# Attention's loop: where the two halves of a score tile stand in TensorE's step

## The reference, cut to what matters

```python
h = _modulate(_layernorm(x), shift_msa, scale_msa)
qkv = h @ W_qkv + b_qkv
q, k, v = (qkv[:, :, 0], qkv[:, :, 1], qkv[:, :, 2])
scores = jnp.einsum('blhd,bmhd->bhlm', q * scale, k)
attn = jax.nn.softmax(scores, axis=-1)
o = jnp.einsum('bhlm,bmhd->blhd', attn, v).reshape(b, l, c)
```

## Time and profile before

| | us |
|---|---|
| time, median of 3 runs | 3148.11 (3144.75 to 3148.4) |
| profiled execution, its own time | 3139.54 |
| its span, first to last instruction | 3137.9 |
| attention's head loop, about | 675 to 1762 of the span |
| first matmul of "scores" to the last | 673.5 to 1755.8 |

### The profile page before, as it was taken

The page is one execution under the profiler, slowest core; times in us unless marked ns, Lnnn a source line. Parts: engine busy times, 40 slices in busy tenths (PEclk is TensorE's granted clock), DMA queues, the critical chain, the costliest instruction groups (busy, mean ns, idle before and its releaser), DMA issues. The chain is left out here.

```text
span 3137.9 us, 51594 instructions
## 1 busy us (share of the span) xinstructions
PE 2823.0 (90%) x16066; PEld 2289.3 (73%) x16066; DVE 1682.8 (54%) x3405; ACT 1450.7 (46%) x1863; POOL 1434.5 (46%) x1065
## 2 busy tenths in 40 slices
PE   7769999979999999999999678689999999999976
PEld 3258787846666666666666467579999999999965
DVE  4456766669998998999899355401111111111125
ACT  2122322249999999999999445511111111111112
POOL 1232323138888888888888544412222222222200
PEclk9779999979999999999999788789999999999988
DMA  6376666644334333343343357792112111111153
GB/s 202 131 262 212 234 217 218 221 116 92 85 87 94 79 92 90 84 92 86 86 93 80 127 171 219 216 320 72 37 37 72 37 37 55 54 37 38 50 163 134
DMA packets 340331, 378.73 MB, mean 121 GB/s; under 512 B 167008, under 2 KB 230120, under 8 KB 340188
## 3 DMA queue, kind: packets, MB, share of 16 engines
q1 hardware_dynamic: 330588, 357.71, 38.3%
q0 software_dynamic: 4224, 9.44, 1.7%
q10 hardware_dynamic: 5380, 9.66, 1.0%
HBM read 226.82 MB, written 158.93 MB: 123 GB/s over the span
## 5 line engine op out<-in xcount | busy, mean ns | idle before, releaser
L815 POOL TENSOR_TENSOR a_pl<-a_pf,a_ph 128x1024 fp32r<-128x1024 f32 x384 | 909.8, 2408 | 23.1 <-ACT a_pf L912 22.9
L843 DVE TENSOR_REDUCE a_mx<-a_psum_s 128x1 f32<-128x512 f32 x992 | 637.8, 684 | 92.4 <-PE a_psum_s L941 88.6
L910 ACT ACTIVATE a_ph<-a_psum_t 128x1024 fp32r<-128x1024 f32 x512 | 526.6, 1028 | 116.2 <-PE a_psum_t L958 108.9
L1562 PE MATMUL m_psum_h<-m_ht,m_w 128*128 128x256 f32 x4032 | 534.9, 284 | 30.3 <-DMA m_w<-w_s 21.0
L1514 POOL TENSOR_TENSOR m_al<-m_af,m_ah 128x256 fp32r<-128x256 f32 x288 | 212.9, 739 | 762.7 <-DVE m_ah L1523 762.7
L1523 DVE CAST m_ah<-m_af 128x256 fp32r<-128x256 f32 x288 | 84.6, 294 | 848.4 <-ACT m_af L1500 848.4
L1562 PEld LDWEIGHTS m_psum_h<-m_ht,m_w 128*128 128x128 f32 x4032 | 508.8, 189 | 34.0 <-issue 33.1
L1500 ACT ACTIVATE m_af<-m_psum_h,m_bias 128x256 f32<-128x256 f32 x288 | 137.3, 477 | 814.2 <-PE m_psum_h L1562 814.2
L1576 PE MATMUL m_psum_y<-m_w,m_ah 128*128 128x288 f32 x2304 | 504.2, 296 | 1.4 <-DVE m_y L1540 1.2
L977 PE MATMUL a_psum_o<-a_ph,a_vs 128*100 128x512 f32 x1024 | 420.0, 410 | 23.8 <-POOL a_pl L815 19.7
L978 PE MATMUL a_psum_o<-a_pl,a_vs 128*100 128x512 f32 x1024 | 404.3, 395 | 0.0
(11 more groups left out here) (225 smaller groups left out, 3106.0 us busy)
## 6 DMA issues: line engine op xcount, KB each, us to landing
a_qs<-q_s SPq DMA_DIRECT2D x192, 144.0 KB
a_ks<-k_s SPq DMA_DIRECT2D x192, 144.0 KB
w_s<-q_ws SPq DMA_DIRECT2D x64, 324.0 KB, 3.4
h_s<-p_ht SPq DMA_DIRECT2D x40, 512.0 KB, 5.1
m_ht<-h_s SPq DMA_DIRECT2D x16, 1280.0 KB, 7.8
v_s<-q_vo SPq DMA_DIRECT2D x64, 288.0 KB, 2.3
a_vs<-v_s SPq DMA_DIRECT2D x128, 144.0 KB, 4.5
q_s<-q_qko SPq DMA_DIRECT2D x32, 512.0 KB, 2.8
```

The source lines that it names most:

```text
L815: pool.tensor_tensor(pl[:, s % RING], pf[:, s % RING], raw(ph[:, s % RING]), ALU.subtract).then_inc(lo_pool, 1)
L843: dve.tensor_reduce(mx[:, u % 2, t, h:h + 1], p_s[:, h * 512:(h + 1) * 512], AX.X, ALU.max) \
L910: act.activation(ph[:, s % RING], p_t[:, s % 2], ACT.Exp, scale=SCALE)
L1562: m = pe.matmul(p_h[:, f % RING, 0:GM], w1[:, k, f * P:(f + 1) * P], ht[:, q, a], start=(i == 0), stop=(i == len(PASSES) - 1))
```

## The change

TensorE's step is written in another order. Before, both halves of score tile s followed the four value products. Now half h0 is the first product of the step, ahead of the scores, and half h1 stands between the value products of the step's first key tile and those of its second. Number, size and operands of the products are the same, and so are all waits; they stand at other places. No other engine's list is changed.

```diff
-                def score_tile(hd, u, i, t):
-                    if t == 0:
+                def score_half(hd, u, i, t, h):
+                    if t == 0 and h == 0:
                         pe.wait_ge(qk_in[u], 16 * QK_LOADS * (i + 1))
-                    for h in range(2):
-                        pe.wait_ge(half_free, 2 * (KT * (hd - 2) + t) + h + 1)
-                        pe.matmul(p_s[:, h * 512:(h + 1) * 512], qs[0:SROWS, u, t * P:(t + 1) * P],
+                    pe.wait_ge(half_free, 2 * (KT * (hd - 2) + t) + h + 1)
+                    pe.matmul(p_s[:, h * 512:(h + 1) * 512], qs[0:SROWS, u, t * P:(t + 1) * P],
...
-                def values(hd, u, i, s):
+                def values(hd, u, i, s, r):
...
+                        ahead = not (last and u >= SLOTS - 2)
+                        tile = (hd + 2, (u + 2) % SLOTS, i + (u + 2) // SLOTS, s)
+                        if ahead:
+                            score_half(*tile, 0)
                         if s + AHEAD < STEPS:
                             scores(hd, u, i, s + AHEAD)
                         elif not (last and u == SLOTS - 1):
                             scores(hd + 1, (u + 1) % SLOTS, i + (u == SLOTS - 1), s + AHEAD - STEPS)
-                        values(hd, u, i, s)
-                        if not (last and u >= SLOTS - 2):
-                            score_tile(hd + 2, (u + 2) % SLOTS, i + (u + 2) // SLOTS, s)
+                        values(hd, u, i, s, 0)
+                        if ahead:
+                            score_half(*tile, 1)
+                        values(hd, u, i, s, 1)
```

More of the change, by code:

```diff
@@ L933, in lead_tile @@
                     score_product(lead_slots[n % 3], u, t)
-                def score_tile(hd, u, i, t):
-                    if t == 0:
+                def score_half(hd, u, i, t, h):
+                    if t == 0 and h == 0:
                         pe.wait_ge(qk_in[u], 16 * QK_LOADS * (i + 1))
-                    for h in range(2):
-                        pe.wait_ge(half_free, 2 * (KT * (hd - 2) + t) + h + 1)
-                        pe.matmul(p_s[:, h * 512:(h + 1) * 512], qs[0:SROWS, u, t * P:(t + 1) * P],
-                                  ks[0:SROWS, u, h * 512:(h + 1) * 512], start=True, stop=True) \
-                          .then_inc(half_ready, 1)
+                    pe.wait_ge(half_free, 2 * (KT * (hd - 2) + t) + h + 1)
+                    pe.matmul(p_s[:, h * 512:(h + 1) * 512], qs[0:SROWS, u, t * P:(t + 1) * P],
+                              ks[0:SROWS, u, h * 512:(h + 1) * 512], start=True, stop=True) \
+                      .then_inc(half_ready, 1)
                 def scores(hd, u, i, s):
@@ L960, in scores @@
                     m.then_inc(t_ready, 1)
-                def values(hd, u, i, s):
+                def values(hd, u, i, s, r):
                     lh, j = divmod(s, PER_LH)
-                    if s == 0:
+                    if s == 0 and r == 0:
                         pe.wait_ge(v_in[u], 16 * V_LOADS * (i + 1))
-                    if j == 0:
+                    if j == 0 and r == 0:
                         pe.wait_ge(o_copied[lh], START + hd)
[L969 to L980, removed]
+                    if r == 0:
+                        n_pool, n_dve = lo_counts(hd, s)
+                        if s in DVE_LO:
+                            pe.wait_ge(lo_dve, n_dve)
+                        else:
+                            pe.wait_ge(lo_pool, n_pool)
+                    t = PAIR * j + r
+                    cols = slice(r * GT, (r + 1) * GT)
+                    pe.matmul(p_o[0:VW, lh], vs[:, u, t], ph[:, s % RING, cols], start=(t == 0), stop=False)
+                    m = pe.matmul(p_o[0:VW, lh], vs[:, u, t], pl[:, s % RING, cols], start=False,
+                                  stop=(t == KT - 1))
+                    if r == PAIR - 1:
+                        m.then_inc(p_free, 1)
                 for n in range(LEAD):
```

## The result

The changed kernel takes **3217.97 us** (median of 4 runs, 3215.41 to 3220.84) where the kernel before takes 3146.43 beside it: a ratio of **1.023**, 95% interval 1.0212 to 1.0247. The forecast was 3213, in a range of 3185 to 3232. All times and ratios here are of runs in the faster of two states; one execution among the experiments, of the kernel with h0 behind the scores in steps 0 and 4, took 10397 us and is left out of them.

The account below looks back on a forecast made before the run. No engine alone but a ring of dependences was taken to set the pace; 47 heads at +0.90 and 14 boundary heads at +1.58 us gave 64.4, which from the median 3148.1 made 3213, range 3185 to 3232.

Parts of the forecast that it names:

- The ring before: Dependences from POOL's split through its low parts, TensorE and DVE back to the split: 16.80 us a head, 17.45 every fourth.
- The two new waits: TensorE's h0 waits for DVE's reductions behind low 1 and low 5: 0.83 us in step 0, 1.1 in step 4.
- A head: One attention head without a loop boundary was to take 17.70 us in place of 16.80, +0.90.
- DVE behind it: After step 4, DVE's 5 h0 at 12.83 releases at 13.57; h0 of step 6 waits only a few hundredths.
- the walk: The prediction's following of one head from the end of low 1 (t = 0), by engine lists and prices: 17.70 us.
- A boundary head: Every fourth head, with ACT's table load (1.33 us, nothing hidden), was to take 19.03 us in place of 17.45, +1.58.
- The restart: After a wait for a half, TensorE was taken to need 0.10 us more, as at the wait for low 1.
- A: Rival: DVE, fed earlier, keeps ahead; no half wait binds, low 1 starts 0.40 us sooner a head; 3129, chance 0.08.
- B: Rival: the new waits fall into TensorE's waits for POOL, whose pace stays; no change, 3148, chance 0.04.
- C: Rival: only one of the two new waits binds; 16.87 us a head, 18.2 at a boundary; 3162, chance 0.07.
- D: Rival: TensorE's clock falls to 1.2 GHz now and then; five such heads cost 61 us more; 3274, chance 0.02.
- The sum: Over the 61 heads between the first and last regular split: 47 x 0.90 + 14 x 1.58 = 64.4 us more.

Follow-up runs that it names:

- the fastest: Against the changed kernel: h0 leads only in steps 3 and 7, behind the scores elsewhere; DVE's low 1 and low 5 between tile halves; 3101.53 us, ratio 0.9872.

## Why the prediction was right, point by point

**The ring before** and its price, 16.80 and 17.45: the experiments with both halves between the value products moved it by the 0.40 that its tail was said to hold. Right.

**The two new waits.** Forecast 0.83 in step 0 and 1.1 in step 4, where h0 then stands; TensorE is idle for 0.86 in step 0. For step 4, in the same head (t = 0 is 1152.72):

```profile
1162.56 0.50 PE L940 MATMUL a_psum_s<-a_ks,a_qs 108*128 108x512 f32 x1 [0.83 <-DVE a_mx L843]
```

The release is right (9.84 after t = 0, forecast 9.82). The 1.1 counted from where h0 would have started, 0.23 after the product ahead of it, to the end of the restart; the row counts from the end of that product, shown 0.17 later, and leaves out the restart of 0.10. So 0.83 and 1.1 are the same wait.

**A head: 17.70 forecast, 17.86 measured.** The mis-sized term is the bullet "DVE behind it": 5 h0 was put at 12.83, releasing step 6 at 13.57 with "a few hundredths" of wait. Its reduction starts at 12.99:

```profile
1163.62 1.34 DVE L843 TENSOR_REDUCE a_mx<-a_psum_s 128x1 f32<-128x512 f32 x2
...
1164.99 0.69 DVE L871 TENSOR_TENSOR a_ob<-a_psum_o,a_ob 36x512 f32<-36x512 f32 x1
...
1165.71 1.97 DVE L843 TENSOR_REDUCE a_mx<-a_psum_s 128x1 f32<-128x512 f32 x3
...
1166.46 0.19 PEld L940 LDWEIGHTS a_psum_s<-a_ks,a_qs 108*128 108x128 f32 x1 [0.34 <-DVE a_mx L843]
...
1166.79 0.64 PE L957 MATMUL a_psum_t<-a_qs,a_ks 110*128 110x512 f32 x2
```

Two small things make up the 0.16. The pair for tile 4 starts where the walk has it (10.90) but lasts 1.34 and not 1.28, so its second reduction begins some 0.06 late. And L871 starts 0.71 behind that reduction, not the 0.60 at which one reduction follows another, and the next operation 0.72 behind L871. So h0 of step 6 is released at 13.74 and waits too; the scores behind it start at 14.07 in place of 13.88, which is 0.19, of which the forecast had allowed 0.03. 0.16 x 47 = 7 us.

**A boundary head: 19.03 forecast, 19.05 measured.** The scores of step 6 feed the exponentials of step 1, and with a table load ahead of step 0's exponentials ACT comes to them only later: ahead of the split at 1118.66 these scores start at 1112.06, and their exponential at 1113.89, with no idle time before it. So the missing 0.16 is hidden there. Right: the 1.19 between 17.86 and 19.05 is the load's 1.33 less what it hides.

**The restart, 0.10.** From h0 at 1153.45 to the scores at 1153.79 it is 0.34 where a matmul takes 0.23, so 0.11. The load of the waiting product started with it, at 1153.45: it had not run ahead. The Trainium skill ("TensorE: Matmul & The Clock Gate", "Step-by-step: what each phase is for") speaks of weight loads pulled ahead of matmuls in flight. In this case a weight load with a semaphore wait of its own was not pulled ahead of that wait.

**The rivals.** A and B did not come. C was priced wrongly: it had "the other's 0.83" come back if only one wait binds, so 16.87; the runs with one low part moved show 17.28 and 17.21. Taking away one of the two waits gives back 0.6 us, not 0.83, since the halves behind it lead too and wait for their own reductions. D, given 0.02 as a whole case, came in small beside the forecast: five heads took 18.9 us in place of 17.86, 5 us in all and not 61, since the clock was low for a part of each head only.

**The sum.** Between the same splits (698.76 to 1809.54) lie 1110.8 us; 1033.45 before; so 77.3, where 64.4 was forecast: 7 from the wait in step 6 and 5 from the clock. The medians are only 71.5 apart, since the profiled execution of before (3139.54) lies 6.9 under its median. So the mechanism was right and the sum 12.9 us short, and that 3213 came within 5 us of 3217.97 is in part luck: by profiled executions the forecast was 3204, against 3217.95.

## What to carry to other kernels

A product that waits for a buffer belongs where nothing urgent stands behind it: an engine's list is strict, so a wait moved to the head of a step becomes a wait of everything in the step. Before moving it, look at the list of the engine that frees the buffer; a long operation ahead of the freeing one is the price. There are two ways out: keep the waiting product behind the urgent ones (3218 to 3113 us here), or move the long operations by one place in the other list (3218 to 3132); both lists fitted to each other gave 3102. The gains of the two don't add up. Where all engines are nine tenths busy and none is the bound, follow one round by hand through the waits, with a price for every step taken from the timeline: here this gave the time of eight other kernels, in which only the order of operations differed, to about 0.3% before they ran; the two changes of the loop's length it missed.

## What the runs showed of the hardware

**The clock fell behind a pause of 1.8 us.** At loop boundaries TensorE of the changed kernel stands 1.8 us ahead of step 0's h0. Behind 5 of its 14 such pauses the granted clock fell to the lower of its two levels (1.2 GHz) for a part of the head, and the head took 1.05 us more; with low 5 alone moved, behind 9 of 14 pauses of 1.79 to 1.80. In the kernel before, and in the kernel where only h0 leads (14 pauses of 1.57), no head stood out. The timeline of such a place in the changed kernel, and its windows (the clock is the third number from the end):

```profile
897.83 0.51 PE L940 MATMUL a_psum_s<-a_ks,a_qs 108*128 108x512 f32 x1 [1.80 <-DVE a_mx L843]
...
899.38 0.63 PE L940 MATMUL a_psum_s<-a_ks,a_qs 108*128 108x512 f32 x1
899.81 0.63 PE L976 MATMUL a_psum_o<-a_ph,a_vs 128*100 128x512 f32 x1
```

```profile
898.00:900.00 2.00, 2.00 (x7) 1.46 (x8) 1.82 (x4) 1.16 (x2) 1.17 (x3) 0.69 0.00 0
900.00:902.00 2.00, 2.00 (x7) 1.43 (x6) 1.89 (x4) 0.77 (x1) 2.00 (x2) 0.50 0.00 0
902.00:904.00 2.00, 2.00 (x10) 1.55 (x9) 1.34 (x3) 1.82 (x2) 1.91 (x1) 0.96 0.13 38
```

Matmuls are 0.43 apart there, not 0.23. The pause that ended at 1117.75, as long (1.79), had no such head behind it; what decides between the two is not shown.

**A loop's table load.** ACT loads its table again at each round of the hardware loop although the function never changes: 15 loads of 1283 ns in attention. A head with a boundary takes 0.65 us more than one without in the kernel before, 1.19 in the changed kernel, 1.07 in the fastest: the load costs what ACT's waits don't hide.

**A longer loop body is not free.** Rounds of eight heads halved the loads and paid for it with 1.5 to 2.9 us at each round's end, beside twelve times as many packets of instructions in attention (73 against 6), and with 28 to 30 us in a stage that nobody had touched.
